# Latent queries of the second half of the samples on other row groups, in the second attention of a two-layer block

## The chip, the core and the metric

The kernel runs as one launch on one core of a Trainium2 chip. The metric is the device time of a run in microseconds. TensorE (PE in the profile, PEld for its weight loads), VectorE (DVE), ScalarE (ACT), GpSimd (POOL) and the DMA queues each work through their own stream of instructions in order, and wait for each other by semaphores.

## The reference, cut to what matters

Two layers of (conditioned convolution, attention, conditioned convolution, feed-forward) over `x` of 32 samples, 32 tokens each, 512 features. The change is in the attention of the second layer, which runs on the output of `_L1_cond_ref`:

```python
q = _rmsnorm(x @ wq_a.T, q_a_ln_w) @ wq_b.T            # 32 heads of 64 + 64
q_nope, q_pe = (q[..., :NOPE], q[..., NOPE:])
ckv_kpe = x @ wkv_a.T
ckv, k_pe = (ckv_kpe[..., :KVR], ckv_kpe[..., KVR:])   # KVR = 32
kv = _rmsnorm(ckv, kv_a_ln_w) @ wkv_b.T
...
q_full = jnp.concatenate([q_nope, q_pe], axis=-1)
k_full = jnp.concatenate([k_nope, jnp.broadcast_to(k_pe[:, :, None, :], (B, S, H, ROPE))], axis=-1)
scores = jnp.einsum('bqhd,bkhd->bhqk', q_full, k_full) * softmax_scale
...
attn = jax.nn.softmax(scores, axis=-1)
out = jnp.einsum('bhqk,bkhd->bqhd', attn, v).reshape(B, S, H * VD)
```

The score of a query and a key is a sum of two products: one of the rotated parts (128 rows in this kernel's layout) and one of the rest, which the kernel has folded into 32 latent rows.

## The kernel before

**Stages.** `attention0`, `ffn(0)`, `attention1` and `ffn(1)` follow each other on every engine; each has a convolution ahead of it. `attention1` takes most of the span from 715 to 905 us of the profiled execution. The order on each engine is written out by hand, and all eight PSUM banks (`ps[:, n, :]`, 512 columns of 4 bytes) are assigned by hand.

**Preparation.** PE forms the folded query weights in banks 4 and 5 (`absorb_keys`, `s1_wq`). ACT copies them to `wql_hi` (`copy_query_weights`, `s1_wqc`), DVE writes what that rounding lost to `wql_lo` (L2318, `s1_wqlo`). PE turns normalised queries, keys and latents (L1421, L1426, L1432); the last of these writes banks 4 and 5 again, so it waits for `s1_wqlo`. ACT copies the turned tiles out (L1754, L1759, `s1_turnc`) and then rounds the rotary query weights of a group (`round_queries`, L1766), POOL writes their low part (`split_queries`, L2533, `s1_wlo`).

**Heads.** The 32 heads are worked in eight groups of four; i counts the groups. For each i:

- `queries(i, tiles)`: eight tiles of 128x512, each of three matmuls on split values (L1451 to L1453, `three`), into a ring of four banks (1, 2, 6, 7); a tile waits until the tile four before it was read. DVE multiplies each with the rotation table (`rotate`, L2332, `s1_rot`).
- `latent_queries(four)`: the same for the latent part, eight tiles for four groups i at a time; i = 0 to 3 ahead of `scores(0)`, i = 4 to 7 in iteration 3. ACT copies them to `q_lat` (`latents_in`, L1775, `s1_lat`). The 32 latent rows of group i stand on partitions 32*(i%4) and up, those of all 32 samples alike; the latent keys `keys_l` stand on all four row groups.
- `scores(i)`: for each half t of the samples (bank 3 + t), 16 products of the rotated parts (L1481, all 128 rows, 32 columns) and 16 of the latent parts (L1487, 32 rows, 32 columns) that add to them. j, one of four samples, picks the 32 columns.
- softmax: DVE turns each half out of PSUM (`soft_pull`, L2061, `s_pull`), POOL adds the mask (L2509), DVE takes the maxima (L2067), POOL subtracts them from the first half (L2515) and DVE from the second (L2360), ACT exponentiates (L1785), DVE sums and inverts (L2072, L2073), POOL scales (L2521), DVE transposes to `flat` (L2342), ACT spreads that into block form (`spread`, L1795, eight instructions).
- `pv(i)` multiplies with the values (L1500), one iteration later; ACT copies the result (`heads_out`, L1805). After the last group `out_tile` (L1528) projects everything.

The order on DVE in an iteration is: both pulls of group i, rotations 0 and 1 of group i + 2, both maxima, the subtraction, rotations 2 and 3, the sums, rotations 4 to 6, both transposes, rotation 7. On PE it is: five query tiles of i + 2, `pv(i - 1)`, three query tiles, `scores(i + 1)`.

Of the kernel before, what the change touches and what calls it, by code (L numbers as in the profile page):

```python
# [29 lines left out]
P = 128  # L30
R = P // C
T = L // R
G = 4
# [178 lines left out]
def build(nc, a, out):  # L212
    ctx = ExitStack()
    with ctx:
# [262 lines left out]
        wql_hi = rounded("wql_hi", [P, 2, GQ, 4 * LAT], "arena", WQL_AT)  # L477
        wql_lo = rounded("wql_lo", [P, 2, GQ, 4 * LAT], "xt", 3 * TOK)
        wq_hi = rounded("wq_hi", [P, NH // GQ, GQ * 2 * ROT], "w_l0", sp0.at)
        wq_lo = rounded("wq_lo", [P, NH // GQ, GQ * 2 * ROT], "arena", 0)  # L480
# [208 lines left out]
        def ring1_tile(name, left, count):  # L689

            ring1_at[name] = (1, 2, 6, 7)[len(ring1_left) % 4]
            ring1_left.append((left, count))

        for n in range(8):
            ring1_tile(("l", 0, n), s1_lat, n + 1)
        for k in range(16):
            ring1_tile(("q", k // 8, k % 8), s1_rot, k + 1)
        for i in range(8):
# [229 lines left out]
        def _(pe):  # L928
# [449 lines left out]
            def attention1():  # L1378
# [85 lines left out]
                def latent_queries(four):  # L1464

                    for n in range(8):
                        bank = ring(("l", four, n))
                        g, half = n // 2, n % 2
                        three(bank, wql_hi[:, four, g, :], wql_lo[:, four, g, :], half).then_inc(s1_l, 1)

                def scores(i):
                    rows = slice(32 * (i % 4), 32 * (i % 4) + 32)
                    pe.wait_ge(s1_rot, 8 * (i + 1))
                    pe.wait_ge(s1_lat, 8 * (i // 4 + 1))
                    for t in range(2):
                        if i:
                            pe.wait_ge(s_pull, SOFT0 + 2 * (i - 1) + t + 1)
                        for m in range(4):
                            for j in range(G):
                                b = (4 * t + m) * G + j  # L1480
                                pe.matmul(ps[32 * j:32 * j + 32, 3 + t, m * P:(m + 1) * P],  # L1481
                                          keys_t[:, b * C:(b + 1) * C], q1[i % 2][:, :, b * C:(b + 1) * C],
                                          start=(m == 0), stop=True, skip_group_check=True)
                        for m in range(4):
                            for j in range(G):
                                b = (4 * t + m) * G + j
                                last = pe.matmul(ps[32 * j:32 * j + 32, 3 + t, m * P:(m + 1) * P],  # L1487
                                                 keys_l[rows, b * C:(b + 1) * C], q_lat[rows, :, b * C:(b + 1) * C],
                                                 **ADD)
                        last.then_inc(s_score, 1)  # L1490

# [15 lines left out]
                pe.wait_ge(s1_wcc, 8)  # L1507

                latent_queries(0)
                queries(0, range(8))  # L1510
                queries(1, range(8))
# [47 lines left out]
        def _(act):  # L1559
# [163 lines left out]
            def attention1():  # L1723
# [6 lines left out]
                def copy_query_weights(q):  # L1730
                    act.wait_ge(s1_wq, q + 1)
                    act.activation(wql_hi[:, q].rearrange("p g (i l) -> p g i l", i=4),
                                   ps[:, 4 + q, :].rearrange("p (i g l) -> p g i l", i=4, g=GQ), ACT.Copy).then_inc(s1_wqc, 1)

# [105 lines left out]
        def _(dve):  # L1840
# [446 lines left out]
            def attention1():  # L2287
# [26 lines left out]
                for q in range(2):  # L2314
                    dve.wait_ge(s1_wqc, q + 1)
                    src = ps[:, 4 + q, :].rearrange("p (i g l) -> p g i l", i=4, g=GQ)
                    split = [w[:, q].rearrange("p g (i l) -> p g i l", i=4) for w in (wql_hi, wql_lo)]
                    dve.tensor_tensor(split[1], src, split[0].bitcast(F32), ALU.subtract).then_inc(s1_wqlo, 1)  # L2318
                for q in range(2):
# [380 lines left out]
```

## Time and profile before

| what | before |
|---|---|
| median of 3 runs | 988.12 us (987.51 to 989.71) |
| profiled execution, whole | 988.84 us |
| its span in the profile | 987.0 us |
| PE busy | 948.4 us, 96% of the span |
| DVE busy | 556.1 us, 56% |
| POOL busy | 469.7 us, 48% |
| ACT busy | 232.8 us, 24% |
| mean granted TensorE clock | 0.996 |

The profiled execution took 1.8 us more than its span, which lies around the profiled instructions. Busy shares are means over stages with different limits; what a change in `attention1` is worth is read from its own stretch. Every fp32 matmul of the program stands as two records of PE in the trace (16 matmuls of L1481 are x32), a matmul on the rounded type as one.

### The profile page before, as it was taken

Reading aid. Unit: us, or ns where it says so; the run is one execution under the profiler, and the core shown is the slowest. Engines: PE = TensorE matmul, PEld = TensorE weight load, DVE = VectorE, ACT = ScalarE, POOL = GpSimd, SP = SyncE. Lnnn points to the kernel's source line nnn. Section 1 sums busy time; section 2 is a strip of 40 time slices with the busy share of each in tenths; the row PEclk is TensorE's granted clock in tenths of the full one; section 3 lists DMA queues with packets and bytes.
Section 4 is the critical chain, followed back from the end, with each engine's and each line's share of the span. In section 5 each row is a group of like instructions: output and inputs, shape, how many; then the busy total and the mean of one; then the engine's idle time right before and its main releaser. Section 6 shows DMA issues by size and latency. Waiting matters only on the chain.

```text
span 987.0 us, 15987 instructions
## 1 busy us (share of the span) xinstructions
PE 948.4 (96%) x6776; PEld 709.6 (72%) x6776; DVE 556.1 (56%) x951; ACT 232.8 (24%) x452; POOL 469.7 (48%) x425
## 2 busy tenths in 40 slices
PE   5899998999999999999999999999989999899997
PEld 2337896877888778887788888847857777446954
DVE  7866747647376573855738744254148969302432
ACT  4602103220222112221111310110161666400010
POOL 7943638497374964748647542301223545220300
PEclk9999999999999999999999999999999999999999
DMA  5792101211012110021100862396460000082002
GB/s 140 167 246 90 59 1 43 75 44 54 2 43 75 43 54 11 34 75 43 54 33 12 207 157 75 77 231 145 151 235 1 3 2 3 2 170 65 4 1 85
DMA packets 36303, 74.30 MB, mean 75 GB/s; under 512 B 13508, under 2 KB 22276, under 8 KB 33156
## 3 DMA queue, kind: packets, MB, share of 16 engines
q1 hardware_dynamic: 35896, 72.89, 26.5%
q8 instruction: 53, 0.87, 0.4%
q10 hardware_dynamic: 336, 0.39, 0.1%
q14 instruction: 18, 0.15, 0.0%
HBM read 66.26 MB, written 7.01 MB: 74 GB/s over the span
## 4 chain that ended last, share of the span: by engine, by line
PE 74%; DVE 9%; POOL 8%; ACT 4%; issue 2%; DMA 1%; SPq 0%; POOLq 0%; DVEq 0%; ACTq 0%
PE ps L1233 14%; PE ps L1165 14%; PE ps L1026 8%; PE ps L1528 6%; PE ps L1310 5%; PE ps L1179 4%; POOL w_lo L2438 3%; DVE arena L2090 3%; ACT acts L1575 2%; PE ps L1451 2%; PE ps L1210 1%; DVE arena L2087 1%; PE ps L1072 1%; PE ps L1453 1%; PE ps L1452 1%
## 5 line engine op out<-in xcount | busy, mean ns | idle before, releaser
L2553 POOL TENSOR_TENSOR arena<-arena 128x512 f32<-128x512 f32 x80 | 103.6, 1296 | 123.0 <-DVE arena L2090 122.9
L1165 PE MATMUL ps<-xt_hi,w_hi 128*128 128x512 f32 x320 | 127.7, 399 | 5.8 <-POOL w_lo L2438 2.7
L1165 PE MATMUL ps<-xt_lo,w_hi 128*128 128x512 f32 x320 | 125.8, 393 | 0.0
L1165 PE MATMUL ps<-xt_hi,w_lo 128*128 128x512 f32 x320 | 124.9, 390 | 0.0
L2090 DVE TENSOR_TENSOR arena<-ps,rope 64x512 f32<-64x512 f32 x160 | 110.2, 689 | 2.2
L2108 DVE TENSOR_TENSOR fresh<-ps,fresh 128x512 f32<-128x512 f32 x56 | 38.7, 691 | 119.7 <-PE ps L1233 119.6
L1233 PE MATMUL ps<-h_hi,wo_lo 128*128 128x512 f32 x224 | 82.1, 395 | 1.6 <-POOL wo_lo L2560 1.6
L1233 PE MATMUL ps<-h_hi,wo_hi 128*128 128x512 f32 x224 | 82.8, 400 | 0.0
L1233 PE MATMUL ps<-h_lo,wo_hi 128*128 128x512 f32 x224 | 81.9, 396 | 0.0
L1165 PEld LDWEIGHTS ps<-xt_hi,w_hi 128*128 128x128 f32 x320 | 60.0, 188 | 24.4 <-DVE arena L2090 4.8
L1675 ACT ACTIVATE h_hi<-ps 128x512 fp32r<-128x512 f32 x64 | 33.1, 604 | 185.9 <-PE ps L1210 185.9
L2438 POOL TENSOR_TENSOR w_lo<-acts,w_hi 128x896 fp32r<-128x896 f32 (+1 forms) x32 | 58.1, 1849 | 35.4 <-ACT w_hi L1645 35.4
L2461 POOL TENSOR_TENSOR xt<-arena 128x512 f32<-128x512 f32 x16 | 20.4, 1272 | 112.1 <-DVE arena L1995 112.1
L1165 PEld LDWEIGHTS ps<-xt_hi,w_lo 128*128 128x128 f32 x320 | 60.1, 188 | 13.2
L1165 PEld LDWEIGHTS ps<-xt_lo,w_hi 128*128 128x128 f32 x320 | 60.2, 188 | 11.8
L2087 DVE TENSOR_TENSOR arena<-ps,rope 128x512 f32<-128x512 f32 x80 | 55.1, 689 | 21.2 <-PE ps L1165 20.0
L2509 POOL TENSOR_TENSOR arena<-arena,causal 128x512 f32<-128x512 f32 x32 | 40.8, 1293 | 30.9 <-DVE arena L2061 30.9
L1026 PE MATMUL ps<-arena,stream 128*128 128x128 f32 x320 | 51.7, 276 | 0.0
L1233 PEld LDWEIGHTS ps<-h_hi,wo_lo 128*128 128x128 f32 x224 | 41.9, 187 | 13.1 <-POOL wo_lo L2560 2.9
L1233 PEld LDWEIGHTS ps<-h_hi,wo_hi 128*128 128x128 f32 x224 | 41.8, 188 | 11.1 <-issue 1.4
L1233 PEld LDWEIGHTS ps<-h_lo,wo_hi 128*128 128x128 f32 x224 | 42.1, 188 | 9.2
L1795 ACT ACTIVATE fresh<-wide 32x512 f32<-32x512 f32 x64 | 40.2, 628 | 23.9 <-DVE wide L2342 23.2
(343 smaller groups left out, 1946.6 us busy)
## 6 DMA issues: line engine op xcount, KB each, us to landing
acts<-in_w_o_dram SPq DMA_DIRECT2D x8, 1024.0 KB, 5.0
arena<-in_a_wo_dram SPq DMA_DIRECT2D x8, 1024.0 KB, 5.7
arena<-kernel_rows SPq DMA_DIRECT2D x11, 512.0 KB, 12.3
acts<-in_w_qkv_dram SPq DMA_DIRECT2D x3, 1792.0 KB, 7.1
acts<-in_w_qkv_dram SPq DMA_DIRECT2D x4, 1280.0 KB, 6.5
w_l<-kernel_rows SPq DMA_DIRECT2D x10, 512.0 KB, 11.3
arena<-level_rows SPq DMA_DIRECT2D x3, 1024.0 KB, 21.2
stream<-in_x_dram SPq DMA_DIRECT2D x4, 512.0 KB, 6.7
```

Source lines behind the costliest of these rows:

```text
L1026: last = pe.matmul(o, stream[:, b, 2 - group:2 - group + T], w, start=(group == 0), stop=(group == 2))
L1165: last = pe.matmul(ps[:, bank, :], w[:, r, cols], x, start=(r == 0 and n == 0), stop=(r == R - 1 and n == 2))
L1179: last = pe.matmul(ps[:, bank, m * 2 * HD:(m + 1) * 2 * HD], x, w[:, r, 5 * HD:7 * HD], start=(r == 0 and n == 0), stop=(r == R - 1 and n ...
L1233: last = pe.matmul(ps[:, bank, :], out_weights(i, g)[w][:, r, :], heads_buffer(i, half)[x][:, g, :], start=(k == 0), stop=(k == len(order) ...
L1310: last = pe.matmul(ps[:, FFN_BANK[k], :], w_main[:, r, r_out, :], xt[:, r, half * HALF:(half + 1) * HALF], start=(r == 0 and not behind), ...
L1528: last = pe.matmul(ps[:, OUT1[n], :], wcomb[:, i, r_out, :], latent(i)[:, half * HALF:(half + 1) * HALF], start=(i == 0), stop=(i == 7))
L1795: last = act.activation(probs1_t[q, 4 * t:4 * t + 4, :, j, :].rearrange("p a g q -> p (a g) q"), flat[q, t, :, :], ACT.Copy)
L2087: dve.tensor_tensor(y[:, 0], x, cos.unsqueeze(1).broadcast_to([P, HALF // C, C]), ALU.mult)
L2090: last = dve.tensor_tensor(y[dst, 1], x[src], sin[src].unsqueeze(1).broadcast_to([64, HALF // C, C]), ALU.mult)
L2438: pool.tensor_tensor(w_lo[:, r, 0:n], src[:, r, 0:n], w_hi[:, r, 0:n].bitcast(F32), ALU.subtract).then_inc(s_wlo, 1)
L2509: pool.tensor_tensor(probs[:, t], probs[:, t], causal[:, :].unsqueeze(1) .broadcast_to([P, 16, C]), ALU.add).then_inc(s_masked, 1)
L2553: pool.tensor_tensor(qk[:, chunk, half * HALF:(half + 1) * HALF], rot[:, k % 2, 0, :], rot[:, k % 2, 1, :], ALU.add).then_inc(s_rope, 1)
```

## The change

The latent part of the second half of the samples (t = 1) moves to the row group two further on: of group i it stands on partitions 32*((i+2)%4) and up. For that ACT and DVE write a second set of folded query weights, `wqs_hi` and `wqs_lo`, in which the two pairs of row groups are exchanged, and `latent_queries` uses it for the tiles of the second half. In `scores` both halves' rotated products now come first, and the latent products of the two halves alternate, t inside j. The first eight query tiles go ahead of the latent ones.

```diff
+        wqs_hi = [rounded(f"wqs_hi{q}", [P, GQ, 4 * LAT], "xt", 2 * q * TOK) for q in range(2)]
+        wqs_lo = [rounded(f"wqs_lo{q}", [P, GQ, 4 * LAT], "xt", (2 * q + 1) * TOK - HALF) for q in range(2)]
+
+        def swapped(q, low):
+
+            made = ps[:, 4 + q, :].rearrange("p (i g l) -> p g i l", i=4, g=GQ)
+            high, rest = (w[q].rearrange("p g (i l) -> p g i l", i=4) for w in (wqs_hi, wqs_lo))
+            for at, of in ((slice(0, 2), slice(2, 4)), (slice(2, 4), slice(0, 2))):
+                yield (rest if low else high)[:, :, at, :], made[:, :, of, :], high[:, :, at, :].bitcast(F32)
+
...
+        for k in range(8):
+            ring1_tile(("q", 0, k), s1_rot, k + 1)
         for n in range(8):
             ring1_tile(("l", 0, n), s1_lat, n + 1)
-        for k in range(16):
-            ring1_tile(("q", k // 8, k % 8), s1_rot, k + 1)
+        for k in range(8, 16):
+            ring1_tile(("q", 1, k % 8), s1_rot, k + 1)
...
-                        three(bank, wql_hi[:, four, g, :], wql_lo[:, four, g, :], half).then_inc(s1_l, 1)
+                        high, low = ((wqs_hi[four], wqs_lo[four]) if half else (wql_hi[:, four], wql_lo[:, four]))
+                        three(bank, high[:, g, :], low[:, g, :], half).then_inc(s1_l, 1)
...
                 def scores(i):
-                    rows = slice(32 * (i % 4), 32 * (i % 4) + 32)
...
-                        for m in range(4):
-                            for j in range(G):
+                    for m in range(4):
+                        for j in range(G):
+                            for t in range(2):
+                                at = 32 * ((i + 2 * t) % 4)
+                                rows = slice(at, at + 32)
                                 b = (4 * t + m) * G + j
                                 last = pe.matmul(ps[32 * j:32 * j + 32, 3 + t, m * P:(m + 1) * P],
                                                  keys_l[rows, b * C:(b + 1) * C], q_lat[rows, :, b * C:(b + 1) * C],
                                                  **ADD)
-                        last.then_inc(s_score, 1)
+                                if m == 3 and j == G - 1:
+                                    last.then_inc(s_score, 1)
...
+                queries(0, range(8))
                 latent_queries(0)
-                queries(0, range(8))
...
                     act.activation(wql_hi[:, q].rearrange("p g (i l) -> p g i l", i=4),
-                                   ps[:, 4 + q, :].rearrange("p (i g l) -> p g i l", i=4, g=GQ), ACT.Copy).then_inc(s1_wqc, 1)
+                                   ps[:, 4 + q, :].rearrange("p (i g l) -> p g i l", i=4, g=GQ), ACT.Copy)
+                    for dst, src, _ in swapped(q, False):
+                        last = act.activation(dst, src, ACT.Copy)
+                    last.then_inc(s1_wqc, 1)
...
-                    dve.tensor_tensor(split[1], src, split[0].bitcast(F32), ALU.subtract).then_inc(s1_wqlo, 1)
+                    dve.tensor_tensor(split[1], src, split[0].bitcast(F32), ALU.subtract)
+                    for dst, src, high in swapped(q, True):
+                        last = dve.tensor_tensor(dst, src, high, ALU.subtract)
+                    last.then_inc(s1_wqlo, 1)
```

What stands on DVE in the preparation, just before the first rotation, before the change (names in square brackets are the semaphores that are waited for; `wql_lo` is the low part of the folded query weights, `qa_lo` that of the query inputs):

```order
473 L2313 COPY w_l<-wide 128x1024 [waits dve_steps]
474 L2318 TENSOR_TENSOR wql_lo<-ps,wql_hi 128x512 [waits l1_absorbed_query_copied] x2
475 L2322 SCALAR_TENSOR_TENSOR qa_lo<-ps,wide,qa_hi 128x512 [waits l1_turned_copied] x2
476 L2332 TENSOR_TENSOR arena<-ps,wide 128x512 [waits l1_query_tile_done,l1_absorbed_output_done]
477 L2332 TENSOR_TENSOR arena<-ps,wide 128x512 [waits l1_query_tile_done] x7
```

and after it:

```order
473 L2332 COPY w_l<-wide 128x1024 [waits dve_steps]
474 L2337 TENSOR_TENSOR wql_lo<-ps,wql_hi 128x512 [waits l1_absorbed_query_copied]
475 L2339 TENSOR_TENSOR wqs_lo_71<-ps,wqs_hi_69 128x4x64 x2
476 L2337 TENSOR_TENSOR wql_lo<-ps,wql_hi 128x512 [waits l1_absorbed_query_copied]
477 L2339 TENSOR_TENSOR wqs_lo_72<-ps,wqs_hi_70 128x4x64 x2
478 L2344 SCALAR_TENSOR_TENSOR qa_lo<-ps,wide,qa_hi 128x512 [waits l1_turned_copied] x2
```

Four subtractions of 256 columns each are new, and they stand ahead of the event that the last turning on PE waits for.

On PE at the end of the preparation, before:

```order
2469 L1432 MATMUL ps<-ident,w_l 128x128 [waits l1_absorbed_query_split,l1_absorbed_query_copied]
2470 L1432 MATMUL ps<-ident,w_l 128x128 x7
2471 L1451 MATMUL ps<-qa_hi,wql_hi 128x512 [waits l1_absorbed_output_copied,l1_query_inputs_split,l1_turned_copied]
2472 L1452 MATMUL ps<-qa_lo,wql_hi 128x512
2473 L1453 MATMUL ps<-qa_hi,wql_lo 128x512
```

and after:

```order
2469 L1444 MATMUL ps<-ident,w_l 128x128 [waits l1_absorbed_query_split,l1_absorbed_query_copied]
2470 L1444 MATMUL ps<-ident,w_l 128x128 x7
2471 L1463 MATMUL ps<-qa_hi,wq_hi 128x512 [waits l1_absorbed_output_copied,l1_query_weights_split,l1_query_inputs_split,l1_turned_copied]
2472 L1464 MATMUL ps<-qa_lo,wq_hi 128x512
2473 L1465 MATMUL ps<-qa_hi,wq_lo 128x512
```

The first tile behind the turning is now one of the rotary queries, and so it waits for `l1_query_weights_split` (`s1_wlo`) as well.

On PE in `scores(0)` and `scores(1)` (L1481 and L1487 before, L1493 and L1502 after), before:

```order
2543 L1481 MATMUL ps<-arena 32x128 [waits l1_latent_queries_copied,l1_rotary_products_done]
2544 L1481 MATMUL ps<-arena 32x128 x15
2545 L1487 MATMUL ps<-wide,arena 32x128 x16
2546 L1481 MATMUL ps<-arena 32x128 x16
2547 L1487 MATMUL ps<-wide,arena 32x128 x16
```

and after:

```order
2543 L1493 MATMUL ps<-arena 32x128 [waits l1_latent_queries_copied,l1_rotary_products_done]
2544 L1493 MATMUL ps<-arena 32x128 x31
2545 L1502 MATMUL ps<-wide,arena 32x128 x32
...
2570 L1493 MATMUL ps<-wide,arena 32x128 [waits scores_turned,l1_latent_queries_copied,l1_rotary_products_done]
2571 L1493 MATMUL ps<-wide,arena 32x128 x15
2572 L1493 MATMUL ps<-wide,arena 32x128 [waits scores_turned]
2573 L1493 MATMUL ps<-wide,arena 32x128 x15
2574 L1502 MATMUL ps<-wide,arena 32x128 x32
```

Four stretches of 16 have become two of 32, and the first half's scores are complete only with the second half's.

## Rows read from the trace of the kernel before

**Rows 1.** The page: busy time of each engine, its share, instructions.

```profile
PE 948.4 (96%) x6776; PEld 709.6 (72%) x6776; DVE 556.1 (56%) x951; ACT 232.8 (24%) x452; POOL 469.7 (48%) x425
```

**Rows 2.** Busy time by window: one iteration (i = 4) in the loop over groups.

```profile
804.32:816.21 11.89, 11.89 (x217) 9.30 (x217) 11.33 (x20) 7.70 (x13) 6.89 (x8) 1.00 0.02 4
```

**Rows 3.** Timeline of DVE, i = 4: start, duration, what, [idle before <-releaser].

```profile
807.51 0.69 DVE L2061 STREAM_TRANSPOSE arena<-ps 128x512 f32<-128x512 f32 x1
808.52 0.72 DVE L2061 STREAM_TRANSPOSE arena<-ps 128x512 f32<-128x512 f32 x1 [0.32 <-PE ps L1487]
...
819.40 0.69 DVE L2061 STREAM_TRANSPOSE arena<-ps 128x512 f32<-128x512 f32 x1
```

**Rows 4.** Timeline of DVE, i = 1.

```profile
766.07 1.29 DVE L2061 STREAM_TRANSPOSE arena<-ps 128x512 f32<-128x512 f32 x2
...
770.89 1.28 DVE L2332 TENSOR_TENSOR wide<-ps,wide 128x512 f32<-128x512 f32 x2
...
775.53 1.30 DVE L2342 STREAM_TRANSPOSE wide<-arena 128x512 f32<-128x512 f32 x2
...
777.33 1.47 DVE L2061 STREAM_TRANSPOSE arena<-ps 128x512 f32<-128x512 f32 x2
```

**Rows 5.** Timeline of PE: `scores(0)`, and the query tile behind it.

```profile
750.99 1.08 PE L1481 MATMUL ps<-arena 128*32 128x128 f32 x32
752.00 1.09 PE L1487 MATMUL ps<-wide,arena 32*32 32x128 f32 x32
...
755.05 0.50 PE L1451 MATMUL ps<-qa_hi,wq_hi 128*128 128x512 f32 x1
```

**Rows 6.** Busy time by window, of L1210, L1026 and L1193 alone.

```profile
188.60:189.90 1.30, 1.17 (x32) 0.98 (x32) 1.00 0.00 0
...
84.87:87.60 2.73, 2.73 (x24) 2.73 (x24) 1.00 0.93 239
...
201.00:202.90 1.90, 1.88 (x64) 1.69 (x64) 1.00 0.00 0
```

**Rows 7.** Timeline of all engines at the end of the preparation.

```profile
730.72 1.28 DVE L2318 TENSOR_TENSOR wql_lo<-ps,wql_hi 128x512 fp32r<-128x512 f32 x2
...
732.02 2.06 ACT L1759 ACTIVATE arena<-ps 128x512 f32<-128x512 f32 x4
732.14 1.06 PE L1432 MATMUL ps<-ident,w_l 128*128 128x128 f32 x8
733.92 1.19 ACT L1766 ACTIVATE wq_hi<-arena 128x512 fp32r<-128x512 f32 x2
734.13 0.50 PE L1451 MATMUL ps<-qa_hi,wql_hi 128*128 128x512 f32 x1 [0.92 <-ACT arena L1759]
...
734.74 2.55 POOL L2533 TENSOR_TENSOR wq_lo<-arena,wq_hi 128x512 fp32r<-128x512 f32 x2 [0.26 <-ACT wq_hi L1766]
```

**Rows 8.** Groups by line and shape: a DVE operation on 256 columns; count, busy us, mean ns.

```profile
L2302 DVE TENSOR_TENSOR w_l<-w_l,wide 128x256 f32<-128x256 f32 x4 | 1.4, 416 | 0.0
```

**Rows 9.** Timeline of DVE, i = 0: rotations 2 and 3.

```profile
759.63 1.27 DVE L2332 TENSOR_TENSOR arena<-ps,wide 128x512 f32<-128x512 f32 x2
```

**Rows 10.** Timeline, i = 2 and 3: the transposes, and the first rotation behind the latent tiles.

```profile
787.16 1.30 DVE L2342 STREAM_TRANSPOSE wide<-arena 128x512 f32<-128x512 f32 x2
...
797.49 1.39 DVE L2332 TENSOR_TENSOR wide<-ps,wide 128x512 f32<-128x512 f32 x2 [6.76 <-PE ps L1453]
```

**Rows 11.** Timeline, the last two groups and the output projection.

```profile
831.31 0.69 DVE L2061 STREAM_TRANSPOSE arena<-ps 128x512 f32<-128x512 f32 x1
...
836.89 1.95 PE L1481 MATMUL ps<-wide,arena 128*32 128x128 f32 x32
...
847.50 2.81 PE L1528 MATMUL ps<-xt,arena 128*128 128x512 f32 x6 [2.07 <-ACT w_l L1805]
```

**Rows 12.** Busy time by window: us, PE, PEld, DVE, ACT, POOL, granted clock, DMA.

```profile
832.20:835.70 3.50, 1.43 (x48) 1.10 (x48) 2.46 (x4) 3.18 (x6) 3.39 (x3) 1.00 0.00 0
835.70:839.10 3.40, 3.40 (x72) 2.98 (x64) 2.85 (x6) 2.08 (x4) 1.75 (x2) 0.50 0.02 5
```

## Prediction

> **What bounds the kernel now.** I began with the page: PE is busy 948.4 us of a span of 987.0 us, so a shorter PE looks like a shorter kernel [rows 1]. The change touches the loop over groups in the second attention alone, so I took one iteration of it by window. PE is busy all 11.89 us of it, but DVE is busy for 11.33 of the same 11.89 us [rows 2]. Two engines bound the loop within 5%; what PE can give back ends where DVE's own work ends.
>
> The timeline of DVE gives its floor. In i = 4 the first pull starts at 807.51 and the next group's at 819.40, 11.89 us later; in between the second pull waits 0.32 us for PE's L1487, the latent products of the second half, and starts at 808.52 [rows 3]. In i = 1 the scores were there in time: both pulls stand as one piece, and from 766.07 to 777.33 the same 20 operations take 11.26 us [rows 4]. 11.26 us is the iteration with no wait for PE, and this is a measured one. Iteration 5 took 819.40 to 831.31, 11.91 us [rows 3, 11].
>
> **What the scores cost, and will cost.** In `scores(0)` the four stretches start at 750.99, 752.00 and so on, and the next query tile at 755.05: 4.06 us, about 1.01 a stretch of 32 records [rows 5]. The rotated products of both halves in one stretch are 64 records of the same shape as L1193, which take 1.88 us in one go [rows 6]. The latent products are 64 records on eight array tiles (two row groups by four column groups) where there were four. No row shows eight tiles at once. For row groups by themselves there is one: L1210 puts 32-row products on four row groups, and its 32 records take 1.17 us with their tail, while 24 records of L1026 on the full array take 2.73 us, 114 ns each, which for 32 would be 3.6 us [rows 6]. Row groups do run together. So the latent stretch is 1.02 us if eight tiles run together (half as many rounds as 64 records on four tiles, hence as long as 32 records now), and 1.88 if they don't. I take 1.02, since L1210 is the nearest row: scores cost 2.90 us of PE, 1.16 less per group.
>
> The Trainium skill, page TensorE: Matmul & The Clock Gate, Part 3, states that 16 tiles of 32x32 reach 10.6 times one tile. No row here shows that many; by it the latent stretch would be the 1.02 us above.
>
> **Where that saving goes.** PE's iteration would be 11.89 - 1.16 = 10.7 us, DVE's 11.26. The loop then follows DVE, and each iteration that waited for PE gains only the difference:
> - i = 4: 11.89 - 11.26 = 0.63; i = 5: 11.91 - 11.26 = 0.65.
> - i = 2: pull to transposes took 777.33 to 787.16, 9.83 us, against 766.07 to 775.53, 9.46 us, in i = 1: 0.37 [rows 4, 10].
> - i = 1: nothing, it is the floor itself. i = 3: nothing; behind the transposes of i = 2 at 787.16 come ACT's spread, the copies of the latent tiles and then rotation 0 at 797.49, for which DVE waits 6.76 us [rows 10]. Scores are not in that chain.
> - i = 6: the chain to the projection at 847.50 is mask, maxima, exponentials, transposes and spread of group 6 from its first pull at 831.31 on; the projection waits for ACT's last copy [rows 11]. It moves with that pull and gains nothing more. The second pull, earlier now, was not late for the mask, which takes the first half first.
> Sum in the loop: 1.65 us.
>
> The Trainium skill, page TensorEngine Tiling (Array Packing), Performance Considerations, warns that packing speeds up TensorE while the copying out of PSUM doesn't follow and may become the bottleneck. The trace agrees: DVE, which reads PSUM here, is 95% busy in this loop [rows 2].
>
> **What the change costs ahead of the loop.** All of this lies on the path, because PE is what everything waits for there.
> - DVE: `wql_lo` starts at 730.72 and takes 1.28 us for two [rows 7]. Four subtractions of 256 columns join; four such operations take 1.4 us [rows 8]. `s1_wqlo` comes at 733.4 instead of 732.0.
> - PE: the turning of the latents (L1432) started at 732.14 and takes 1.06 [rows 7]; it now starts at 733.4 and ends at about 734.5.
> - ACT: its four copies ran from 732.02 to 734.08 [rows 7]. The last now starts at 734.55 and ends at 735.15. Only then does it round the query weights of group 0, about 0.6 us: 735.7 (before: 733.92 on).
> - POOL: `split_queries(0)` starts 0.14 us behind ACT and takes 1.3 (half of 2.55) [rows 7]: 735.85 to 737.15. POOL's clearing of `made` ends before, at 734.5, and hides nothing new.
> - PE: the rotary tiles are first now, and wait for that split: 737.2 instead of 734.13 [rows 7]. Before, eight latent tiles (5.6 us) covered the split.
> PE starts 3.1 us late. Bounds: if DVE's additions cost nothing, the split alone ends at 734.74 + 1.3 = 736.04, +1.9; if each is as long as one of 512 columns (0.6), +4.1. The additions on ACT (four copies of 256 columns) lie ahead of waits for PE's L1405 and cost nothing here; uncovered they would be 1.4 us.
>
> From there 24 tiles follow without a stop, as before, so `scores(0)` starts 3.1 us late too. Then from its start to rotation 2 of i = 0: before 750.99 to 759.63, 8.64 us [rows 5, 9]. After: 2.90 for the scores, 0.1 to the pull, and then the pattern of i = 1, 766.07 to 770.89, 4.82 us [rows 4], 7.82 in all. That gives back 0.82; the first pull is not hidden behind the second half's products any more, or it would be more.
>
> Sum without the clock: +3.1 - 0.82 - 1.65 = **+0.6 us**.
>
> **The clock.** The granted clock fell to half, 1.2 GHz, once in this attention, for 835.70 to 839.10, behind 3.5 us in which PE was busy for 1.43 us [rows 12]. A stretch of L1481 took 1.95 us there, 1.08 at 2.4 GHz [rows 5, 11], so 3.4 us at the lower level cost about 3.4 x 0.45 = 1.5 us of PE. Before, PE's pause at 734.13 was 0.92 us [rows 7] and the clock stayed. After, PE stands from about 732.2 to 733.4 and from 734.5 to 737.2, with 1.1 us of work in 5 us: less than in the row behind which the clock fell. So I expect it to fall, in or right behind this gap, and the first query tiles to run at half clock for part or all of such a stretch. I take +1.3 (0 to 1.6); DVE only follows PE there, so it is paid in full.
>
> The total is +1.9 us. The profiled execution, 988.84 us with its span of 987.0, lies 0.7 above the median; I count from the median, 988.12: **990.0 us**.
>
> **Rivals.**
> 1. *The clock stays up in the gap.* For it: it also survived other pauses of about 1 us, as the one at 734.13 [rows 7]. Against: the gap is far emptier. Time: 988.12 + 0.6 = 988.7. Chance 0.22.
> 2. *The eight tiles don't overlap*, only four run at a time. Scores cost 3.76 us, both halves complete only then, and DVE's first pull is no longer covered. The loop follows PE again at 11.89 - 0.30 = 11.6 us, and group 6's first pull, which stood at 831.31 ahead of the second half's products, comes about a full latent stretch later. Against the forecast: `scores(0)` 0.86 later, i = 4 and i = 5 0.34 longer each, and in i = 2 and 4 PE late by another 0.5 each: about +3.0. Time 993 with the clock's loss, 991.7 without. Chance 0.10.
> 3. *Faster: DVE is not the floor*, the loop follows PE at 10.7 us. It needs DVE's 20 operations to fit there; they'd have to lose more than the one wait that i = 1 shows gone. Six iterations at -1.16, less the 3.1 and the clock: 988.12 - 7.0 - 0.8 + 3.1 + 1.3 = 984.7. It decides from the point at which DVE's busy time per iteration falls under 11 us; at 11.33 [rows 2] nothing speaks for that. Chance 0.06.
> The forecast (clock falls, tiles overlap): 0.62.
>
> **How the numbers follow.** A difference of 0.2%, 2.0 us, is about what a measurement of this kernel can tell from none; the edges are 986.1 and 990.1. The forecast at 990.0 with the bounds of the late start (-1.2, +1.0) lies on the upper edge: 0.53 of it same, 0.47 slower. Rival 1 is same but for a little, rival 2 slower, rival 3 faster; some faster is left for what I overlook. Slower 0.29 + 0.01 + 0.10 = 0.40, same 0.53, faster 0.07. The range takes in rival 1 with its lower bound (987.5) and the forecast with its upper bounds, and reaches toward rival 2: 987.2 to 992.3.
>
> **What would show each step.** In the profile after: 64 latent records in about 1.0 us (rival 2: 1.9); the two pulls of i = 4 and 5 in one piece and 11.26 us to the next; the first rotary tile at about 3.1 us behind where the first latent tile stood, released by POOL; a granted clock of 0.5 somewhere in the 6 us behind it; the projection 1.5 to 2.5 us late. I am wrong if the split is not what releases PE, if PE then stops in the 24 tiles, or if DVE's pulls still wait.

## The result, and the profile after

The changed kernel takes 992.86 us, median of 7 runs (991.39 to 995.89), against 988.12 (986.69 to 990.84, 7 runs on the same chip) of the kernel before: ratio 1.0052, 95% interval 1.0033 to 1.0071. It is slower, by 4.7 us, and lies 0.6 us above the forecast range of 987.2 to 992.3. Its profiled execution took 992.86 us too, with a span of 991.1 us and a mean granted clock of 0.989 where before had 0.996.

The page of the changed kernel has the line that answers to [rows 1]: busy time, share, instructions.

```profile
PE 945.7 (95%) x6776; PEld 707.1 (71%) x6776; DVE 554.9 (56%) x955; ACT 234.3 (24%) x456; POOL 469.2 (47%) x425
```

PE is busy 2.7 us less than before in a span that is 4.1 us longer, so it stands idle for 6.8 us more; and some of its busy time is work at half clock.

The end of the preparation, timeline of all engines, against [rows 7] (start, duration, what, [idle before <-releaser]):

```profile
728.40 0.68 DVE L2337 TENSOR_TENSOR wql_lo<-ps,wql_hi 128x512 fp32r<-128x512 f32 x1
...
731.15 1.07 PE L1444 MATMUL ps<-ident,w_l 128*128 128x128 f32 x8 [1.31 <-DVE wqs_lo L2339]
...
732.79 1.15 ACT L1785 ACTIVATE wq_hi<-arena 128x512 fp32r<-128x512 f32 x2
733.57 2.50 POOL L2555 TENSOR_TENSOR wq_lo<-arena,wq_hi 128x512 fp32r<-128x512 f32 x2 [1.39 <-ACT wq_hi L1785]
...
734.98 0.77 PE L1463 MATMUL ps<-qa_hi,wq_hi 128*128 128x512 f32 x1 [2.76 <-POOL wq_lo L2555]
```

DVE's `wql_lo` stands at 728.40, at 730.72 before [rows 7]: this execution is 2.32 us ahead when it comes to the change. That is not the change's doing. The executions of four kernels with the same work up to there (the changed one, e1, e8 and e2) have that instruction at 728.40, 729.98, 730.31 and 731.80. Part of it is a piece of half clock at the start of the program that before's execution has and after's lacks: over all fourteen traces of this study, the five without it have the instruction at 728.40 to 729.09, the nine with it at 729.98 to 731.80 (windows of before, then of after: us, busy PE, PEld, DVE, ACT, POOL, granted clock, DMA share, GB/s):

```profile
43.80:47.20 3.40, 3.14 (x4) 1.51 (x5) 2.98 (x6) 0.00 (x0) 3.09 (x5) 0.50 1.05 208
```

```profile
43.80:47.20 3.40, 3.40 (x10) 1.28 (x10) 3.37 (x7) 0.00 (x0) 3.17 (x4) 1.00 1.08 211
```

So I add 2.32 to each of after's times before I compare. The first tile then starts 734.98 + 2.32 - 734.13 = 3.17 us late.

Timeline of PE, `scores(0)`, against [rows 5]:

```profile
753.17 1.95 PE L1493 MATMUL ps<-arena 128*32 128x128 f32 x64
755.05 1.17 PE L1502 MATMUL ps<-wide,arena 32*32 32x128 f32 x64
756.15 0.50 PE L1463 MATMUL ps<-qa_hi,wq_hi 128*128 128x512 f32 x1
```

From the first product to the next tile it is 2.98 us instead of 4.06, and the 64 latent records take 1.10 us from their first start to the next tile's.

Timeline of DVE: the pulls, and the first rotation behind the second set of latent tiles, against [rows 3, 4, 10, 11]:

```profile
767.52 1.29 DVE L2080 STREAM_TRANSPOSE arena<-ps 128x512 f32<-128x512 f32 x2
778.77 1.29 DVE L2080 STREAM_TRANSPOSE arena<-ps 128x512 f32<-128x512 f32 x2
790.01 1.29 DVE L2080 STREAM_TRANSPOSE arena<-ps 128x512 f32<-128x512 f32 x2
800.09 1.38 DVE L2354 TENSOR_TENSOR wide<-ps,wide 128x512 f32<-128x512 f32 x2 [8.79 <-PE ps L1465]
...
810.11 1.30 DVE L2080 STREAM_TRANSPOSE arena<-ps 128x512 f32<-128x512 f32 x2
...
821.37 1.29 DVE L2080 STREAM_TRANSPOSE arena<-ps 128x512 f32<-128x512 f32 x2
...
832.62 1.29 DVE L2080 STREAM_TRANSPOSE arena<-ps 128x512 f32<-128x512 f32 x2
```

Every pair of pulls is one piece, and the iterations 1, 2, 4 and 5 take 11.25, 11.24, 11.26 and 11.25 us. That is the DVE floor. The exception is i = 3: DVE waits 8.79 us where it waited 6.76, and the pull of group 4 comes 20.10 us behind that of group 3, against 18.55 before (from this row of DVE to 807.51 [rows 3]):

```profile
788.96 0.69 DVE L2061 STREAM_TRANSPOSE arena<-ps 128x512 f32<-128x512 f32 x1
```

Busy time by window, the same columns as above, against [rows 12]:

```profile
728.00:734.50 6.50, 2.91 (x24) 2.46 (x24) 4.33 (x9) 4.92 (x9) 4.45 (x2) 1.00 0.28 116
734.50:738.00 3.50, 3.02 (x7) 2.47 (x8) 0.78 (x2) 0.00 (x0) 1.57 (x2) 0.51 0.00 0
...
792.30:796.00 3.70, 1.25 (x5) 1.05 (x6) 0.00 (x0) 3.65 (x7) 0.99 (x1) 1.00 0.00 0
796.00:799.40 3.40, 3.40 (x9) 2.65 (x8) 0.00 (x0) 2.01 (x5) 0.00 (x0) 0.50 0.00 0
829.00:833.50 4.50, 2.84 (x128) 2.37 (x120) 4.50 (x9) 1.90 (x4) 1.59 (x3) 1.00 0.01 4
833.50:840.30 6.80, 5.50 (x100) 4.71 (x104) 4.88 (x9) 5.38 (x9) 5.05 (x5) 0.50 0.01 2
840.40:847.20 6.80, 4.18 (x160) 3.17 (x152) 4.07 (x7) 5.35 (x9) 3.84 (x4) 1.00 0.01 4
847.20:854.00 6.80, 4.83 (x6) 2.18 (x7) 3.36 (x7) 5.33 (x10) 2.06 (x2) 0.50 0.00 0
```

The granted clock is at 1.2 GHz in four stretches of this attention, 20.4 us in all, where before had one of 3.4 us. Each lies behind a stretch in which PE had pauses. The releasers of these pauses are in the timeline of PE:

```profile
794.75 0.50 PE L1463 MATMUL ps<-qa_hi,wql_hi 128*128 128x512 f32 x1 [2.53 <-ACT wide L1794]
...
834.16 1.93 PE L1516 MATMUL ps<-fresh,wide 128*32 128x128 f32 x32 [2.32 <-ACT fresh L1814]
...
849.17 6.08 PE L1544 MATMUL ps<-xt,arena 128*128 128x512 f32 x8 [2.43 <-ACT w_l L1824]
```

Before, the pause ahead of the fifth latent tile was 0.77 us:

```profile
793.70 0.50 PE L1451 MATMUL ps<-qa_hi,wql_hi 128*128 128x512 f32 x1 [0.77 <-ACT wide L1775]
```

Eight records of the output projection take 6.08 us, most of it at the lower clock; before they took 3.67.

### The profile page after: what moved, and what is told of

Read it like the earlier page. It is cut to its first block, busy times and chain, and to the rows that moved or that the text cites. A ratio compares the mean times of both kernels' runs of the same rounds, so it can differ in the third digit from the quotient of the medians.

```text
span 991.1 us, 15995 instructions
## 1 busy us (share of the span) xinstructions
PE 945.7 (95%) x6776; PEld 707.1 (71%) x6776; DVE 554.9 (56%) x955; ACT 234.3 (24%) x456; POOL 469.2 (47%) x425
## 4 chain that ended last, share of the span: by engine, by line
PE 72%; DVE 11%; POOL 9%; ACT 3%; issue 3%; DMA 1%; SPq 0%; POOLq 0%; DVEq 0%; ACTq 0%
PE ps L1245 14%; PE ps L1177 14%; PE ps L1038 8%; PE ps L1544 6%; PE ps L1322 5%; PE ps L1191 4%; POOL w_lo L2460 3%; DVE arena L2109 3%; POOL arena L2531 2%; ACT acts L1591 2%; PE ps L1222 1%; PE ps L985 1%; DVE arena L2106 1%; PE ps L1084 1%; PE ps L1304 1%
## 5 line engine op out<-in xcount | busy, mean ns | idle before, releaser
L2483 POOL TENSOR_TENSOR xt<-arena 128x512 f32<-128x512 f32 x16 | 20.4, 1273 | 112.2 <-DVE arena L2014 112.2
```

## The experiments

Ratios are against runs of the kernel before on the same chip in the same session (median 989.53 us of 26 runs for the first four, 989.84 of 29 for the next four, 989.83 of 23 for the last four). Each group of four ran on another chip, so kernels are compared by their ratios and not by their microseconds. A filler is a 128x128 matmul on the identity into a bank that is free then; nobody reads its result, and the kernel's own work stays whole.

| kernel | mean clock of its runs | median us | ratio to before, 95% |
|---|---|---|---|
| changed kernel | 0.989 | 992.86 | 1.0052 (1.0033 to 1.0071) |
| e1 fillers at all three places | 0.998 | 988.46 | 0.9988 (0.9977 to 0.9998) |
| e2 latent tiles first | 0.991 | 991.34 | 1.0013 (1.0001 to 1.0025) |
| e3 scores in the old order | 0.994 | 992.69 | 1.0035 (1.0021 to 1.0048) |
| e4 latent halves in turn | 0.990 | 993.91 | 1.0043 (1.0028 to 1.0057) |
| e5 fillers at the start only | 0.992 | 992.93 | 1.0028 (1.0017 to 1.0039) |
| e6 fillers at the latent tiles only | 0.991 | 993.21 | 1.0037 (1.0024 to 1.0051) |
| e7 fillers at the end only | 0.996 | 990.87 | 1.0011 (1.0001 to 1.0020) |
| e8 second weight set written late | 0.992 | 989.05 | 0.9991 (0.9977 to 1.0006) |
| e9 = e8, fillers at latents and end | 0.998 | 986.00 | 0.9960 (0.9946 to 0.9975) |
| e10 = before, fillers as e9 | 0.998 | 989.54 | 0.9997 (0.9988 to 1.0005) |
| e11 = e8, DVE copies four latent tiles | 0.993 | 986.09 | 0.9961 (0.9948 to 0.9975) |
| e12 = e11, fillers at the end | 0.999 | 981.82 | 0.9924 (0.9911 to 0.9936) |

My theory after the first comparison: the loop did what was forecast, and the missing microseconds are pauses of PE behind which the clock fell. The rivals: the rotary tiles at the front are the cost; or the new score order itself is.

**e1: fillers in the pauses.** The changed kernel with this added, in front of the waits at three places (5 and 11 around the last turning, 9 ahead of the fifth latent tile of the second set, 4 ahead of each half of `pv(5)` and `pv(6)`, 9 ahead of the projection):

```diff
+                def fill(bank, count):
+                    for _ in range(count):
+                        pe.matmul(ps[:, bank, 0:P], ident[:, :], ident[:, :], start=True, stop=True)
...
+                        if four and n == 4:
+                            pe.wait_ge(s_pull, SOFT0 + 8)
+                            fill(3, 9)
```

> The changed kernel with small matmuls of the identity (0.22 us each) added into PSUM banks that are free at that moment, in PE's pauses: 5 and 11 of them at the end of the preparation, 9 ahead of the fifth latent tile of i = 4 to 7, 4 ahead of each half of the last two value products, 9 ahead of the output projection. Their results are overwritten. Theory (the granted clock fell in these pauses and that cost about 5 us): 4 to 5 us faster than the changed kernel, 988 to 989, and no stretch at half clock between 728 and 860 us. Rival (the late start and the waits alone cost it, the clock falls beside the path): no gain, 993 or up to 1 us more, since the added matmuls stand ahead of real ones.

Measured: 0.9988, so 0.0064 (6.3 us) under the changed kernel. The granted clock is 1.00 in all of this attention. The timelines of DVE and of PE at the start, at the fifth latent tile and at the projection:

```profile
729.98 0.68 DVE L2351 TENSOR_TENSOR wql_lo<-ps,wql_hi 128x512 fp32r<-128x512 f32 x1
```

```profile
736.55 0.47 PE L1469 MATMUL ps<-qa_hi,wq_hi 128*128 128x512 f32 x1 [0.30 <-POOL wq_lo L2569]
...
792.27 2.17 PE L1443 MATMUL ps<-ident 128*128 128x128 f32 x18
794.95 0.50 PE L1469 MATMUL ps<-qa_hi,wql_hi 128*128 128x512 f32 x1 [0.51 <-ACT wide L1808]
...
847.40 3.60 PE L1557 MATMUL ps<-xt,arena 128*128 128x512 f32 x8
```

This execution is 730.72 - 729.98 = 0.74 us ahead at `wql_lo`. Its first tile starts 736.55 + 0.74 - 734.13 = 3.16 us late, so the fillers did not shorten the way to it; its projection starts 847.40 + 0.74 - 847.50 = 0.64 us late. The sum that the prediction gave without the clock is +0.6. It holds step by step: the pulls of groups 1, 3, 4, 5 and 6 are 2.39, 1.98, 1.97, 1.33 and 0.67 us late in this trace, and the terms of the prediction without the clock give 2.28, 1.91, 1.91, 1.28 and 0.63.

**e2, e3, e4: one part of the change undone.** e2 puts the eight latent tiles ahead of the rotary ones again, as before the change. e3 keeps the new row groups and has the old order of products, half after half. e4 has both rotated halves first, but then the latent products of one half after the other, so that only four array tiles have work at a time:

```diff
-                    for m in range(4):
-                        for j in range(G):
-                            for t in range(2):
+                    for t in range(2):
+                        for m in range(4):
+                            for j in range(G):
```

> The changed kernel with the latent query tiles ahead of the rotary ones again, as before the change. PE's first tile then waits for the query inputs' low part and ACT's last copy, not for POOL's split: it should stand 1.1 us later than before the change where the changed kernel stands 3.1 later. Theory (late start plus clock): 2 us from the start, and up to 1.3 more if the clock stays up in the shorter pause: 989.6 to 990.9. Rival (the order of the tiles has no part in it): 993.

> The changed kernel with the products in the old order: rotated and latent ones of the first half, then of the second, four tiles at a time, the second half's latents still on the other row groups. The preparation is that of the changed kernel. Theory (what the shorter scores save, 2.5 us, is taken back by clock falls that PE's longer pauses bring): 992 to 993, within 1 us of the changed kernel, with one fall in the preparation and not in the latent tiles of i = 3. Rival (the scores' saving is kept, the falls are chance): 2.5 us slower than the changed kernel, 995.4.

> The changed kernel with t outside m and j in the latent products: all 16 of the first half, then all 16 of the second, so four tiles run at a time. A latent stretch of 64 records takes 1.9 us, not 1.1. Theory (PE has room in the loop, DVE is the floor at 11.26 us, but first pulls are no longer covered): iterations of 11.6 us, about 3 us slower than the changed kernel from the waits, less up to 3 us of clock that the shorter pauses keep: 993 to 996. Rival (eight tiles at once are worth nothing, since PE waits anyway): 993 with iterations of 11.26.

Measured: e2 1.0013, e3 1.0035, e4 1.0043. In e2 the turning still waits for DVE; with `wql_lo` at 731.80, 1.08 us behind before's, its first tile, at 736.35, is 1.14 us late instead of 3.17, and the clock does not fall behind it. So the four subtractions ahead of the turning cost 1.1 us of the late start, and the new order of the tiles, which waits for POOL's split, the other 2.0. Timeline of PE:

```profile
734.55 1.06 PE L1442 MATMUL ps<-ident,w_l 128*128 128x128 f32 x8 [1.31 <-DVE wqs_lo L2337]
...
736.35 0.50 PE L1461 MATMUL ps<-qa_hi,wql_hi 128*128 128x512 f32 x1 [0.74 <-ACT arena L1776]
```

In e3 the loop is as slow as before. Timeline of DVE:

```profile
791.66 0.70 DVE L2078 STREAM_TRANSPOSE arena<-ps 128x512 f32<-128x512 f32 x1
...
800.17 1.39 DVE L2352 TENSOR_TENSOR wide<-ps,wide 128x512 f32<-128x512 f32 x2 [6.74 <-PE ps L1465]
...
810.19 0.70 DVE L2078 STREAM_TRANSPOSE arena<-ps 128x512 f32<-128x512 f32 x1
811.20 0.72 DVE L2078 STREAM_TRANSPOSE arena<-ps 128x512 f32<-128x512 f32 x1 [0.31 <-PE ps L1501]
822.08 0.70 DVE L2078 STREAM_TRANSPOSE arena<-ps 128x512 f32<-128x512 f32 x1
```

Iteration 4 takes 11.89 us again, with the wait of 0.31 us for the second half. And i = 3 takes 18.53 us, with PE's clock up, against 20.10 in the changed kernel. e3 lacks the loop's gain of 1.7 us and lacks this fall, which took 1.55, and ends within the changed kernel's interval. e4 tells how little the loop asks of PE, and its outcome is not the expected 11.6 us an iteration but that of its rival, 11.26. Timeline of PE, and of DVE in i = 4:

```profile
755.64 1.58 PE L1502 MATMUL ps<-wide,arena 32*32 32x128 f32 x64
757.16 0.50 PE L1463 MATMUL ps<-qa_hi,wq_hi 128*128 128x512 f32 x1
```

```profile
810.81 1.29 DVE L2080 STREAM_TRANSPOSE arena<-ps 128x512 f32<-128x512 f32 x2
822.07 1.29 DVE L2080 STREAM_TRANSPOSE arena<-ps 128x512 f32<-128x512 f32 x2
```

With half the tiles at work the 64 records take 1.52 us to the next tile instead of 1.10, and the iteration is 11.26 us all the same. The stretch was expected at 1.9. Before, the two stretches of 32 records took 1.02 us each (752.00 to 753.02 and 754.03 to 755.05), 2.04 together. So of the 0.94 us that the changed kernel saves in a group's latent products, 0.52 come from joining the two stretches and only 0.42 from eight tiles at once. e4's time cannot be told from the changed kernel's, so eight tiles at once, for which the second weight set is written, gain nothing here that was measured. Whether the joined order does as much on the old row groups, without that set, no run shows.

**e5, e6, e7: the fillers of e1 at one place each.**

> The changed kernel with matmuls on the identity, whose result nobody reads, in TensorE's pauses at the end of the preparation only (5 ahead of the last turning, 11 behind it). If half clock there costs what the traces suggest (scores(0) came 1.3 us later than the late start explains), the first fall is gone and the time is 1.3 us under the changed kernel's 992.9: about 991.6. If the clock is no cause, it is 992.9 and the loop starts no earlier. The falls at the fifth latent tile and at the end stay.

> The changed kernel with 9 such matmuls ahead of the fifth latent tile of the second set only. Theory: the first rotation behind the latent tiles came 1.6 us later than the pull explains, because the latent and rotary tiles behind a pause of 2.5 us ran at half clock; with the pause filled it is 991.3. Rival (the delay is the chain of ACT's copies, at any clock): 992.9.

> The changed kernel with 4 such matmuls ahead of each half of the last two products with the values, and 9 ahead of the output projection only. Theory: the last groups and the projection ran for 13.6 us at half clock, and the part of it on the path (the projection's first six tiles and the wait ahead of them) cost about 2.2 us: 990.7. Rival (the projection waits for the chain of softmax at any clock): 992.9.

Measured against the changed kernel's 1.0052: e5 0.0024 less (2.4 us), e6 0.0015 (1.5 us), e7 0.0041 (4.1 us). The interval of each such difference is about 0.002 wide to either side, so e7 alone is told from nothing, e5 just, e6 not by its time. The three sum to 8.0 us where e1 measured 6.3; within these intervals that is the same.

e5's trace shows something that I had not expected: its clock stays up at the fifth latent tile, where no filler stands. The execution that was traced is the fastest of e5's 12 (989.70 us, their median 992.93). Busy time by window:

```profile
791.30:795.00 3.70, 1.22 (x5) 1.05 (x6) 0.00 (x0) 3.65 (x7) 1.04 (x1) 1.00 0.00 0
795.00:798.40 3.40, 3.40 (x16) 2.73 (x15) 0.84 (x2) 2.38 (x5) 0.00 (x0) 1.00 0.00 0
```

PE's pause there is 2.50 us, with 1.22 us of work in 3.7 us, the same as in the changed kernel's execution (2.53 and 1.25), and there the clock fell. The same pause is followed by a fall in one execution and not in another. Over all traces with the eight copies on ACT but e10's, which follows below, what the clock does there sets how far the pull of group 4 comes behind that of group 3:

| traces | pause of PE ahead of the fifth tile, us | clock behind it | pull 3 to pull 4, us |
|---|---|---|---|
| changed kernel, e2, e4, e8 | 2.53, 2.51, 2.12, 2.50 | fell | 20.10, 20.09, 20.12, 20.09 |
| e5, e7 | 2.50, 2.52 | stayed | 18.54, 18.54 |
| e1, e6, e9 | filled | stayed | 18.54, 18.55, 18.55 |
| before, e3 | 0.77, 0.77 | stayed | 18.55, 18.53 |

So a fall there costs 1.55 us, and without one the pause costs nothing. e7 has no filler there either, so a part of its 4.1 us may be falls at this place that its runs happened not to have.

**e8: the start made cheap.** The second low set goes behind the query inputs on DVE, with further counts of the same semaphore that the second latent tile waits for; the latents are turned into banks 6 and 7, which hold nothing that DVE still reads; latent tiles first as in e2. No filler.

```diff
-                pe.wait_ge(s1_wqc, 2)
-                pe.wait_ge(s1_wqlo, 2)
+                pe.wait_ge(s1_wcc, 8)
                 for m in range(NTILE):
-                    last = pe.transpose(ps[:, 4 + m // 4, (m % 4) * P:(m % 4 + 1) * P],
+                    last = pe.transpose(ps[:, 6 + m // 4, (m % 4) * P:(m % 4 + 1) * P],
...
+                        if n < 2:
+                            pe.wait_ge(s1_wqlo, 2 + half * (four + 1))
```

> The changed kernel with a cheaper preparation and no matmul added: the latents are turned into banks 6 and 7, which don't hold the folded query weights, so the turning waits for no subtraction; the low parts of the second weight set are written behind the first set and the query inputs; the latent tiles come ahead of the rotary ones again. The late start of 3.1 us and the clock's fall behind it (1.3 us) should go: the first tile starts within 0.5 us of where it stood in the kernel before. That is 992.9 - 4.4 = 988.5 if all else stays. The falls at the fifth latent tile and at the end stay. If instead the start is not what costs (the old order of the tiles alone gave 991.3 with the late turning), it stays at 991.

Measured: 0.9991, which is 0.0061 under the changed kernel, more than the expected 4.4 us by an amount within the interval. Timeline of all engines:

```profile
730.31 1.28 DVE L2336 TENSOR_TENSOR wql_lo<-ps,wql_hi 128x512 fp32r<-128x512 f32 x2
...
732.83 1.41 DVE L2344 TENSOR_TENSOR wqs_lo<-ps,wqs_hi 128x256 fp32r<-128x256 f32 x4
...
733.74 0.50 PE L1460 MATMUL ps<-qa_hi,wql_hi 128*128 128x512 f32 x1 [1.12 <-ACT arena L1777]
```

The first tile is at 733.74 + 0.41 - 734.13 = 0.02 us: the late start is gone whole, 1.1 us of it by the turning that no longer waits for the subtractions and 2.0 by the order of the tiles (e2). The four subtractions take 1.41 us, as [rows 8] gave, but behind the work that PE waits for. The 12 runs of e8 range widely, and their granted clock goes with it: 991.29 to 992.21 us in the four at 0.988, 985.72 to 988.93 in the five at 0.995. The 78 runs of the kernel before show the same: 16 at 0.991 have a median of 991.1, 19 at 0.996 one of 988.1.

**e9 and e10: fillers on e8, and on the kernel before.** Those at the fifth latent tile and at the end.

> The cheaper preparation (latents turned into banks 6 and 7, second low set written late, latents first) with the fillers at the fifth latent tile and at the end. Theory: this is the change's own gain in the loop, with neither the late start nor the half clock: the cheaper preparation alone ran at 0.9991 of before, its mean clock 0.9915, and each 0.001 of clock was worth 0.6 us in these runs; at 0.998 that is about 3.5 us less: ratio 0.995 to 0.997. Rival (the fillers themselves cost what they save, or the loop gained nothing): 0.999.

> The kernel before the change with the same fillers at the fifth latent tile and at the end: what they are worth where the change is not. Its half-clock stretches in this attention are few (one of 3.4 us, off the path, in the profiled run). Theory (the change brought its own clock falls): ratio 0.998 to 1.000. Rival (the fillers help any such kernel as much): 0.995.

Measured: e9 0.9960, e10 0.9997. The fillers take 3.1 us off e8 and nothing that can be told off the kernel before, although they raise its mean clock from 0.994 to 0.998. That does not show that the falls of the kernel before lie off its path. Its own runs are 3.0 us apart between 0.991 and 0.996, and the fillers cost time in it: nine of them stand ahead of a fifth latent tile that before waited for only 0.77 us, and hold it up by 0.98 us, counted from the pull of group 3. Timeline of DVE in e10, i = 3 and the next pull:

```profile
788.78 0.69 DVE L2072 STREAM_TRANSPOSE arena<-ps 128x512 f32<-128x512 f32 x1
...
808.27 0.70 DVE L2072 STREAM_TRANSPOSE arena<-ps 128x512 f32<-128x512 f32 x1
```

That is 19.49 us, 0.94 more than before's 18.55. So e10 is a gain of clock less a cost of about 0.9 us, and how much of the kernel before's time is clock stays open.

**e11 and e12: useful work in the pause.** In i = 3, DVE copies the first four latent tiles, in the stretch in which it waited 8.8 us, and ACT the last four.

```diff
                     soft_pull(i, SOFT0, p)
+                    for n in range(4 if i == 3 else 0):
+                        dve.wait_ge(s1_l, 8 + n + 1)
+                        dve.tensor_copy(q_lat[:, n // 2, n % 2 * HALF:(n % 2 + 1) * HALF], ps[:, ring1_at["l", 1, n], :])\
+                            .then_inc(s1_latd, 1)
```

> The cheaper preparation, and no matmul added; the first four latent tiles of the second set are copied by DVE, which waits 8.8 us there, and only the last four by ACT. Theory: TensorE's pause of 2.5 us at the fifth latent tile goes by useful work, its clock stays up there, and the next pull comes 2 to 4 us earlier: 0.9991 - 0.003 = 0.996. Rival (ACT's spread and the softmax behind it set the pull, not the latent tiles): no change, 0.999.

> The same with the fillers at the end (4, 4 and 9 matmuls). Theory: the falls at the end cost 2 to 3 us there too: ratio 0.993 to 0.995. Rival: as without them, 0.996.

Measured: e11 0.9961, as expected, and e12 0.9924, a little under the expected 0.993 to 0.995: the fillers at the end take 3.7 us more. Timeline of DVE in e11:

```profile
787.19 1.29 DVE L2082 STREAM_TRANSPOSE arena<-ps 128x512 f32<-128x512 f32 x2
788.41 2.45 DVE L2380 COPY wide<-ps 128x512 f32<-128x512 f32 x4
792.95 1.39 DVE L2357 TENSOR_TENSOR wide<-ps,wide 128x512 f32<-128x512 f32 x2 [2.09 <-PE ps L1463]
...
802.97 1.30 DVE L2082 STREAM_TRANSPOSE arena<-ps 128x512 f32<-128x512 f32 x2
```

The pull of group 4 comes 15.78 us behind that of group 3, 2.8 us less than with a mere filler (18.55), and PE does not stop at the fifth latent tile. e12 is the best kernel of this study, 0.76% under the kernel before. Busy time by window, i = 3 and the end, with the clock up in both:

```profile
786.00:796.00 10.00, 10.00 (x99) 7.71 (x81) 7.87 (x14) 7.11 (x12) 3.84 (x4) 1.00 0.01 2
824.00:841.00 17.00, 13.73 (x362) 11.70 (x348) 13.23 (x23) 14.35 (x24) 9.53 (x9) 1.00 0.01 3
```

## Why the prediction was wrong

990.0 us was forecast, with "same" as the likeliest outcome at 0.53 and "slower" at 0.40, and 992.86 came, 4.7 us above before where 1.9 were forecast. This table follows its steps through the trace. "Late" is after's time plus 2.32 minus before's.

| place | before | after | late | step, measured | step, forecast |
|---|---|---|---|---|---|
| first tile | 734.13 | 734.98 | +3.17 | +3.17 | +3.1 |
| `scores(0)` | 750.99 | 753.17 | +4.50 | +1.33 | +1.3 (clock) |
| pull of group 1 | 766.07 | 767.52 | +3.77 | -0.73 | -0.82 |
| pull of group 3 | 788.96 | 790.01 | +3.37 | -0.40 | -0.37 |
| pull of group 4 | 807.51 | 810.11 | +4.92 | +1.55 | 0 |
| pull of group 5 | 819.40 | 821.37 | +4.29 | -0.63 | -0.63 |
| pull of group 6 | 831.31 | 832.62 | +3.63 | -0.66 | -0.65 |
| projection | 847.50 | 849.17 | +3.99 | +0.36 | 0 |
| end of the span | 987.0 | 991.1 | +6.4 | +2.4 | 0 |

The +6.4 us holds for these two executions once their different starts are taken out; the medians differ by 4.7.

**What held.** The late start, its cause (DVE's four subtractions ahead of the turning, then ACT's rounding and POOL's split, uncovered) and its size; e8 moved the subtractions, the turning and the tiles and it was gone. The length of the latent stretch: 1.10 us for 64 records against a forecast of 1.02. The reason given for it holds in part: the prediction put this whole saving down to eight tiles at once and had 1.88 us for four, and e4 measures 1.52, so half of it is the joined order; for the same reason rival 2 was priced too high. The DVE floor: four iterations at 11.24 to 11.26 us, and e4's longer scores changed none of it, which rules out rival 3. The Trainium skill, page TensorE: Matmul & The Clock Gate, Part 3, states that small matmuls on different tiles of the array run at the same time. The trace agrees for eight tiles, with 1.10 us against 1.52 on four; no run shows sixteen. The 10.6 times for sixteen tiles that the prediction took from it is less than sixteen, so it does not by itself give the forecast 1.02 us, which takes eight tiles to be twice as fast as four. The sum without the clock, +0.6: e1 measures +0.64 at the projection in its trace.

**The step that failed** is the term "The clock". It counted one fall, in the gap at the start, and gave it +1.3, which is what the trace shows. I looked for pauses only where the change adds a wait. But the change takes 1.08 us of work from PE in every group and gives the loop 0.66 us at most; the rest becomes a pause of PE wherever it already waits for another engine. In i = 3 the fifth latent tile, which waits for ACT's copy, starts 3.37 us late (793.70 before, 794.75 after), as late as the pull, but PE is through with the tiles ahead of it only 1.61 late: a pause of 0.77 us became 2.53, the clock fell behind it, and the rotations that DVE waits for were written at half clock, +1.55. "Scores are not in that chain" was true of the work and not of the clock. At the end the pauses ahead of `pv(5)`, `pv(6)` and the projection were there before too, 2.07 us ahead of the latter [rows 11]; after, the fall came at 847.2 and the projection's first 4.85 us ran at 1.2 GHz; its first eight records took 2.4 us more than before. Rows 12 had shown a fall in this tail already, and I priced it as a past event and not as one that can come back elsewhere. The term should have been 1.3 + 1.55 + 2.4, some 5.3 us in this execution, where it was 1.3. That half clock is the missing part is shown by e1 (all fillers, -6.3 us) and e7 (end only, -4.1 us); the share of i = 3 is shown by the traces (20.09 to 20.12 us in the four that fell, 18.54 in e1, e5 and e7, whose clock stayed up) and not by e6's time.

**What stays open.** Why the clock falls behind a pause in one execution and stays up behind the same pause in another. And how much of the fall at the projection is the change's doing: e3, with the old order of products and a pause of 1.89 us there, has a fall of 3.4 us in its projection too, and so has every other trace without fillers at the end but before's. The 2.4 us at the projection are therefore a chance, not a certainty, of the changed kernel: its 7 runs lie at 0.986 to 0.993 and 991.39 to 995.89 us. The profile of before with its 0.996 stands above the mean of that kernel; its 78 later runs average 0.994. A forecast from one execution compares one draw, and I should have given the clock a range up to some 5 us rather than 1.6.

## What to carry to other kernels

Where a loop is bound by two engines within some per cent, as here, work taken from TensorE turns into pauses of TensorE, and these are priced by the granted clock of what runs behind them: list every wait of TensorE on the path after the change, not the new ones alone. Shorten such a pause with work that someone needs (e11: four copies moved to an idle DVE, -2.8 us) before filling it with matmuls that nobody reads (e9), which cost time where the pause is shorter than they are (e10: 0.94 us). And new preparation work goes behind the event that the next engine waits for: the four subtractions cost 1.1 us ahead of it (e2) and nothing behind it (e8).

## What the runs showed that I had not expected

- Eight array tiles of 32x32 (two row groups by four column groups) work side by side: 64 records of 32x128 in 1.10 us, against 1.52 us with four tiles at a time (e4) and 2 x 1.02 us in two stretches before. More of the saving comes from the joined order than from the further tiles.
- The time of a run goes with its granted clock: in the kernel before, runs at 0.991 and at 0.996 differ by 3.0 us (991.1 and 988.1, medians of 16 and 19 runs).
- The same pause of PE, 2.5 us with 1.2 us of work in 3.7 us, had a fall behind it in the changed kernel's profiled execution and none in e5's and e7's.
- Fillers that raise the mean clock need not gain: on the kernel before, 0.994 to 0.998 and a ratio of 0.9997, with 0.94 us lost to the fillers at the fifth latent tile (e10).
